# Vision tower on one core: in every attention step VectorE's three operations on scores stand together

## The reference, cut to what matters

```python
h = tok(x)                                  # 64 images x 37 tokens x 256
h = h + attention0(layernorm(h))            # 16 heads of 16, causal, with bias
h = h + experts(layernorm(h))               # a shared expert and 2 of 7 routed
h = h + attention1(layernorm(h))            # 16 heads of 16, causal
h = h + ffn(layernorm(h))

def attention(x):                           # both layers
    scores = q @ k.T / sqrt(16) + bias      # masked above the diagonal
    p = softmax(scores)                     # exp(scores - max) / sum
    return (p @ v) @ Wo + bo
```

## Time and profile before

| what | value |
|---|---|
| median of 3 runs | 1016.62 us (1014.36 to 1017.39) |
| the profiled execution | 1017.2 us, its span 1015.4 us |
| mean granted clock of TensorE | 0.988 |
| busy: TensorE, its weight loads | 953.8 us, 879.7 us |
| busy: VectorE, ScalarE, GpSimd | 719.8, 660.7, 360.4 us |
| attention of layer 0, layer 1 | about 69 to 227 us, 719 to 888 us of the span |

### The profile page before, as it was taken

The page is one execution under the profiler, slowest core; times in us unless marked ns, Lnnn a source line. Parts: engine busy times, 40 slices in busy tenths (PEclk is TensorE's granted clock), DMA queues, the critical chain, the costliest instruction groups (busy, mean ns, idle before and its releaser), DMA issues.

```text
span 1015.4 us, 29001 instructions
## 1 busy us (share of the span) xinstructions
PE 953.8 (94%) x10725; PEld 879.7 (87%) x10726; DVE 719.8 (71%) x1403; ACT 660.7 (65%) x1206; POOL 360.4 (35%) x284
## 2 busy tenths in 40 slices
PE   5979999988999997999999999999899999899998
PEld 5967888868899996999999999999778888699998
DVE  3546667766566666899999999997467777666643
ACT  3336677865465645687777777777577678565652
POOL 1154454465576750111111211131556544611210
PEclk9999999999999999999999999999899999999999
DMA  6630000007311134111111211122611100000000
GB/s 238 236 111 3 3 3 3 3 3 298 110 39 38 39 74 192 36 37 36 36 38 34 63 35 41 36 61 68 167 26 27 27 3 3 3 13 13 26 25 25
DMA packets 30995, 57.69 MB, mean 57 GB/s; under 512 B 13218, under 2 KB 22434, under 8 KB 29740
## 3 DMA queue, kind: packets, MB, share of 16 engines
q1 hardware_dynamic: 16000, 39.42, 12.3%
q0 software_dynamic: 13664, 15.25, 5.3%
q10 hardware_dynamic: 1228, 1.57, 0.5%
HBM read 41.43 MB, written 14.67 MB: 55 GB/s over the span
## 4 chain that ended last, share of the span: by engine, by line
PE 76%; ACT 6%; DVE 5%; issue 5%; DMA 5%; POOL 2%; SPq 1%; DVEq 0%; ACTq 0%; POOLq 0%
PE ps L1495 19%; PE ps L1500 17%; PE ps L1502 16%; PE ps L1501 16%; PE ps L1652 3%; PE ps L1902 3%; PE ps L1641 2%; DMA x_in<-in_xT_dram 1%; DMA dn_i<-in_dn_dram 1%; DMA routed_in<-prs,slot 1%; PE ps L1790 1%; POOL routed_in L556 1%; ACT RTs L741 1%; ACT RTs L739 1%; DVE Hd L1204 1%
## 5 line engine op out<-in xcount | busy, mean ns | idle before, releaser
L1390 DVE TENSOR_TENSOR tile_w<-arena,tile_w 128x704 fp32r<-128x704 f32 x129 | 142.7, 1134 | 24.4 <-ACT tile_w L933 21.9
L585 POOL DMA_INDIRECT routed_out<-yt,tile_to x43 | 42.8, 996 | 262.1 <-DVE yt L1408 261.8
L933 ACT ACTIVATE tile_w<-arena 128x704 fp32r x129 | 122.5, 986 | 0.6 <-issue 0.6
L1500 PE MATMUL ps<-tile_w,xTs 128*128 128x352 f32 x344 | 114.9, 334 | 4.5 <-DVE tile_w L1390 2.4
L1502 PE MATMUL ps<-tile_w,xTs 128*128 128x352 f32 x344 | 111.3, 324 | 0.0
L1501 PE MATMUL ps<-tile_w,xTs 128*128 128x352 f32 x344 | 110.9, 322 | 0.0
L456 POOL TENSOR_TENSOR Km<-KT,cst 128x592 f32<-128x592 f32 x64 | 75.8, 1186 | 72.8 <-ACT KT L717 36.7
L1209 DVE TENSOR_TENSOR Hf_lo<-Hd,Hf_hi 128x296 fp32r<-128x296 f32 x96 | 51.0, 531 | 57.5 <-ACT Hf_hi L854 57.5
L1500 PE MATMUL ps<-xf_hi,gu_lo 128*128 128x296 f32 x272 | 84.1, 309 | 0.4 <-ACT prs L688 0.4
L1082 DVE SCALAR_TENSOR_TENSOR ps<-ps,bias 128x592 f32<-128x592 f32 x64 | 50.1, 782 | 46.0 <-PE ps L1495 46.0
L854 ACT ACTIVATE Hf_hi<-Hd 128x296 fp32r<-128x296 f32 x96 | 43.2, 450 | 60.6 <-DVE Hd L1204 60.6
(11 more groups left out here) (233 smaller groups left out, 3080.7 us busy)
## 6 DMA issues: line engine op xcount, KB each, us to landing
arena<-in_ew_dram SPq DMA_DIRECT2D x5, 2176.0 KB, 13.3
x_in<-in_xT_dram SPq DMA_DIRECT2D x7, 888.0 KB, 6.0
xt<-routed_in SPq DMA_DIRECT2D x43, 129.0 KB, 2.0
arena<-in_ew_dram POOLq DMA_DIRECT2D x2, 2176.0 KB, 11.4
yg<-routed_out SPq DMA_DIRECT2D x6, 512.0 KB
out_dram<-h SPq DMA_DIRECT2D x7, 296.0 KB, 2.7
routed_in<-zero_x SPq DMA_DIRECT2D x12, 129.0 KB, 4.1
gu_i<-in_gu_dram SPq DMA_DIRECT2D x1, 1536.0 KB, 10.5
```

Source lines behind the costliest of these rows:

```text
L933: act.activation(tile_w[half][0][:, cols], gate_up_of(w, half)[:, cols], ACT.Copy).then_inc(s.wh, 1)
L1390: dve.tensor_tensor(tile_w[half][1][:, cols], gate_up_of(w, half)[:, cols], tile_w[half][0][:, cols].bitcast(F32), ALU.subtract).then_inc( ...
L1500: pe.matmul(out_, w[1], x[0], start=start, stop=False)
```

## The change

Only VectorE's `step` in attention is written in another order. Each waits for the same semaphores as before. In quarter 0 `greatest` now comes before `normalise`, and `centred` before the first `values`; the two routed additions of layer 1 stay ahead of `centred`. In quarters 1, 2 and 3 `scaled`, `greatest` and `centred` stand directly behind each other, and `normalise`, then `centre` or `residual`, then `values` follow.

```diff
                 def step(g, b, X):
                     n = 4 * g
                     scaled(n + 1, 1)
+                    greatest(n + 1, 1)
                     if not X.first:
                         normalise(g - 1, n - 1, 3, 1 - b, X.bank("O3"))
-                    greatest(n + 1, 1)
                     if X.comb:
                         add_routed(g + 2, 0, X.bank("comb0"))
                         add_routed(g + 2, 1, X.bank("comb1"))
+                    centred(n + 1, 1)
                     values(n, 0, X.bank("V0"))
-                    centred(n + 1, 1)
                     values(n + 1, 1, X.bank("V1"))
 
                     scaled(n + 2, 2)
+                    greatest(n + 2, 2)
+                    centred(n + 2, 2)
                     normalise(g, n, 0, b, X.bank("O0"))
-                    greatest(n + 2, 2)
                     if X.last:
                         dve.wait_ge(f.xn, FREE + 1)
                     centre(*norm_ahead(l, g, X), X.bank("mean"))
-                    centred(n + 2, 2)
                     values(n + 2, 2, X.bank("V2"))
 
                     scaled(n + 3, 3)
+                    greatest(n + 3, 3)
+                    centred(n + 3, 3)
                     normalise(g, n + 1, 1, b, X.bank("O1"))
-                    greatest(n + 3, 3)
                     if not X.first:
                         residual(g - 1, 0, X.bank("out0p"))
-                    centred(n + 3, 3)
                     values(n + 3, 3, X.bank("V3"))
 
                     if not X.last:
                         scaled(n + 4, 0)
+                        greatest(n + 4, 0)
+                        centred(n + 4, 0)
                     normalise(g, n + 2, 2, b, X.bank("O2"))
-                    if not X.last:
-                        greatest(n + 4, 0)
-                    if not X.last:
-                        centred(n + 4, 0)
                     if not X.first:
                         residual(g - 1, 1, X.bank("out1p"))
                 over_body(dve, l, step)
```

## The result

The changed kernel takes 1003.09 us (median of 4 runs, 1000.32 to 1005.6) against 1016.33 before (4 runs): a ratio of 0.9871, with a 95% interval of 0.984 to 0.9902. A second series of it gave 1001.61 us, a ratio of 0.9863 (0.9845 to 0.9881). The forecast was 1002.3 us, with a range of 999 to 1011.

A forecast was written before the change was run, and what follows sets the result against it. TensorE, busy 953.8 of 1015.4 us, was taken as the bound, its waits on late `centred` as the gain. Terms 4.6 + 3.15 + 3.4 + 1.2 + 0.9 + 1.1, called 14.3, took 1016.62 to 1002.3 us; range 999 to 1011.

The forecast's parts named there:

- The row of three: VectorE's `scaled`, `greatest`, `centred` back to back: 2.40 us from start of `scaled` to end of `centred`.
- nothing arrives: Rival: the three operations don't run that close, or later stages give the lead back; 1016.6 us, chance 0.06.
- the working of 3.35 us: Length of VectorE's three operations by the skill's drain rule; hardly anything would be gained; 2 in 100.
- Quarter 3 of the middle groups: Groups 1 to 5, both layers: `scores` begins earlier, net 0.46 us a group, 4.6 in all.
- The 0.06 taken off: Quarter 0: `normalise` behind `greatest` ends later and `V1` waits for it, 0.06 us lost a group.
- The end of group 0: TensorE's long wait before `scores`, with no output projection to fill it: gains 1.5 us in layer 0, 1.2 in layer 1.
- The cap by `km`: Last group: GpSimd's `km` becomes last before `scores`, so 3.4 us gained for what would be 5.5.
- Tail: End of each layer: `deviation`, then GpSimd's `xn`, move up 0.6 us, together 1.2.
- Routed additions: Layer 1: `add_routed` comes 0.77 us earlier, `proj0` no longer waits; some 0.22 each, four count, 0.9 us.
- Clock: Layer 0, 90 to 94 us: the fall of the granted clock goes with the idle before it, 1.1 us gained.
- Covered moves: Later `normalise` in quarters 1 to 3 and other moved calls cost 0; `proj3` in quarter 1 has 0.8 us cover.
- slower: Rival: late `normalise` exceeds its cover and stops TensorE in quarters 1 to 3; 1021.4 us, chance 0.04.

The follow-up runs named there:

- experiment 1: Kernel before the change, with only quarter 3 in the new order (`normalise` behind `greatest` and `centred`): 1008.07 us, ratio 0.9929.
- experiment 4: Changed kernel, but in quarter 3 of group 0 `normalise` stands ahead of `greatest` again: 1001.98 us, ratio 0.9876.
- experiment 5: Changed kernel, with GpSimd's last-group `km` and `lower_out` issued before the long FFN weight operation: 999.9 us, ratio 0.9851.
- experiment 2: Kernel before the change, with only quarter 0 in the new order: 1011.67 us, ratio 0.9964.
- experiment 3: Kernel before the change, with only quarters 1 and 2 in the new order: 1009.76 us, ratio 0.9936.
- experiment 6: Changed kernel, with `normalise` moved to the very end of quarter 1, behind `centre` and `values`: 1011.03 us, ratio 0.9952.
- experiment 7: Changed kernel, with `scaled`, `greatest` and `centred` together in quarter 0 too, `normalise` behind them: 1008.87 us, ratio 0.993.

## Why the prediction was right

The forecast of 1002.3 us was for the right reasons but for two sizes and one cause.

- **The row of three, 2.40 us:** 2.38 to 2.40 in quarters 1 to 3 (2.5 and more in quarter 0, where `normalise` stands between). With it the rival "nothing arrives" falls: starts are 0.81 us apart for operations of 0.77. The Trainium skill's drain after every operation (VectorE: DVE Perf Modes, The DRAIN you can't avoid) does not show here as a stretch added to the duration. The same section says that "a next op that is not held starts earlier", which the working of 3.35 us left out and with which these rows agree.
- **Quarter 3 of the middle groups, 0.46 a group:** 0.50 measured, by pair and in experiment 1 alone. The 0.06 taken off for a later `normalise` in quarter 0 does not show. The end of group 0, 1.5 and 1.2: 1.74 and 1.70 measured, and experiment 4 took 0.94 of it back in each layer by moving one operation.
- **The cap by `km`, 3.4:** 3.25 measured (1.90 and 1.35), with `km` as releaser in both layers, and experiment 5 removed it. This term was right because GpSimd's queue was followed past its weight operation; the earlier trace rows alone would have promised 5.5.
- **Tail, 0.6 and 0.6:** from the start of the last `scaled` to GpSimd's `xn` it is 4.85 and 4.86 us, before 5.43 and 5.44.
- **Routed additions, 0.22 a group:** mis-sized. They measured 0.48 (experiment 2; 0.49 to 0.51 in the changed kernel), thus 2.0 and not 0.9. The step that failed is "0.5 us of idle weight loads, some 0.22 of the matmuls": I took the matmuls' idle, whose ends are modelled, and the time was the weight loads' 0.48.
- **Clock, 1.1:** the wrong cause. The step "with the idle nearly gone I take the fall as gone too" has its result (the window from 90 to 94 us shows 1.00) and not its reason: experiment 2 keeps 1.84 us of idle, experiment 4 has 1.23, and neither has the fall. The one profile of the kernel before has it; whether that kernel's other executions do is not known. The words "the trace shows a fall only here" misread that trace too: its granted clock is 0.50 from 230.6 to 234 us, from 264.7 to 268 and from 404.7 to 408, and 0.51 from 722 to 729. Activity ahead of a fall is what the Trainium skill's rule is about (TensorE: Matmul & The Clock Gate, Part 1: The HAM clock gate); these runs show only that this idle alone did not decide it.
- **Covered moves, 0:** right in the middle groups. In group 0, which has no output projection as filling work in quarter 2, `proj4`'s weight load waits 0.38 us for `normalise` and 0.17 us are lost in each layer, the sign that was named for "slower"; experiment 3 has it too. In quarter 1 the cover of 0.8 us measured 0.74, and experiment 6 went past it and paid one to one. The order in quarter 0, taken as given, is what kept the gain (experiment 7).
- **Not in the prediction:** 2.1 us lost between pairs 10 and 11 of layer 1, where a code packet came to lie behind a load. "No DMA is issued by any moved call: 0" was true and not enough, since stages that move in time can bring loads and code packets into another order.

Place by place the sum stood too low by 0.4 in the middle groups of layer 0, by 1.2 in those of layer 1 (1.1 of it the additions) and by 0.5 at the end of group 0 of layer 1; the unforeseen 2.1 went the other way. If the two pieces of clock are peculiar to the profiled execution of the kernel before, which is assumed and not shown, the median loses them: 14.8 - 0.9 - 0.4 = 13.5, between the 13.2 and 14.5 of the two series. That the forecast came out within 1 us is in part such cancelling.

## What to carry to other kernels

When a bank is handed back by the last of several operations on an in-order engine, put those directly behind each other, and price the gain by the waiting engine's own next work, place by place; then look at which queue is last after that, as here GpSimd's behind a long weight operation. What is pushed back must have a cover, and the cover can be read from the trace before the change: the distance from its new end to the first instruction that needs its buffer. Take distances from start to start of one repeated instruction; idle in brackets can understate a wait by half.

## What the runs showed of the hardware

A stop of TensorE of 1.96 us inside a run of like matmuls, with "issue" as releaser and no semaphore to wait for, came with a code packet of 16 KB that arrived 2.5 us behind the start of a load of 592 KB; it came back in the second profile (1.68 us) and was 0.31 with the load moved. In seven profiles the stop and that order of packet and load go together, in five neither is there. Changes of VectorE's order alone brought it (experiments 1 and 3), though not every one did (2 and 4). And an idle of TensorE of 1.84 us at the same place of the program was followed by a lower granted clock (0.58) in one profile and by full clock (1.00) in another.
